# A fused group-norm, sign convolution and involution kernel: lane swaps in place of statistics matmuls, a second sum bank, whole copies on ScalarE, and patch loads put in another order

## What is computed

```python
x = x + conv3x3(sign(gn(x)), sign(weight)) * scale      # gn: mean and variance over each pair of channels
r   = relu(bn(w_r @ gn(x) + b_r))                       # 64 channels to 16
ker = w_s @ r + b_s                                     # 16 channels to 49 taps x 16 groups, for every pixel
for ki in range(7):
    for kj in range(7):                                 # the "involution": a 7x7 kernel of its own at every pixel
        out = out + pad(gn(x))[:, ki:ki+56, kj:kj+56] * ker[ki*7+kj]     # one kernel for the 4 channels of a group
x = x + out
```

## Time and profile before

| | us |
|---|---|
| median of 3 runs | 2095.22 (2088.94 to 2097.33) |
| profiled execution, its own time | 2100.36 |
| its span, first to last instruction | 2097.7 |
| PE busy | 1703.9 (81%) |
| DVE busy | 1350.2 (64%) |
| ACT busy | 1056.1 (50%) |
| POOL busy | 1025.0 (49%) |
| granted TensorE clock, mean | 0.914 |

### The profile page before, as it was taken

One profiled execution on the slowest core, in us unless ns is written; L12 is line 12 of the kernel. 1 busy time (PEld: TensorE's weight loads), 2 busy tenths in 40 slices (PEclk: granted clock), 3 DMA queues, 4 the chain that ended last, 5 costly groups with the idle time before them and its releaser, 6 DMA issues.

```text
span 2097.7 us, 39368 instructions
## 1 busy us (share of the span) xinstructions
PE 1703.9 (81%) x15168; PEld 752.8 (36%) x15168; DVE 1350.2 (64%) x1652; ACT 1056.1 (50%) x758; POOL 1025.0 (49%) x905
## 2 busy tenths in 40 slices
PE   3487887888788788887878888788887878878775
PEld 2243333433333333333333333333333433333332
DVE  5376665757667575776657667576766757667574
ACT  2354555544555445555545555445555545554453
POOL 2145455444545444555454545445555454544573
PEclk8798999999989899999989999899998999989997
DMA  4679789797898978899797997978799798997894
GB/s 102 171 184 225 202 229 227 183 232 198 223 210 206 230 192 222 199 236 238 185 234 185 236 225 200 227 195 229 194 233 230 190 228 198 235 225 185 211 259 110
DMA packets 224283, 436.47 MB, mean 208 GB/s; under 512 B 89214, under 2 KB 136751, under 8 KB 219951
## 3 DMA queue, kind: packets, MB, share of 16 engines
q1 hardware_dynamic: 148832, 382.57, 73.7%
q10 hardware_dynamic: 75264, 51.39, 9.8%
HBM read 336.06 MB, written 84.93 MB: 201 GB/s over the span
## 4 chain that ended last, share of the span: by engine, by line
issue 38%; POOL 37%; PE 9%; SPq 7%; DMA 3%; DVE 2%; ACT 2%; POOLq 0%; ACTq 0%; DVEq 0%
POOL folded L369 37%; SPq L307 5%; PE ybank L564 3%; PE ybank L583 2%; DMA patches<-parts_dram 2%; PE obank L594 1%; DVE prod L820 1%; SPq L289 1%; DMA relu<-blocks 1%; PE ybank L554 1%; PE ybank L525 1%; PE obank L601 1%; PE ybank L615 1%; ACT blocks L458 0%; ACT blocks L416 0%
## 5 line engine op out<-in xcount | busy, mean ns | idle before, releaser
L369 POOL TENSOR_TENSOR folded<-prod 128x448 f32<-128x448 f32 x896 | 1013.3, 1144 | 1051.0 <-DVE prod L820 1040.6
L820 DVE TENSOR_TENSOR prod<-ybank,relu 128x896 f32<-128x896 f32 x896 | 956.8, 1086 | 314.2 <-PE ybank L583 240.2
L583 PE MATMUL ybank<-patches,wspan 128*64 128x448 f16 x7168 | 845.5, 374 | 157.2 <-DVE prod L820 128.5
L436 ACT ACTIVATE patches<-patches 64x1792 f16<-64x1792 f16 x448 | 740.9, 1698 | 450.0 <-DMA patches<-parts_dram 228.5
L583 PEld LDWEIGHTS ybank<-patches,wspan 128*64 128x64 f16 x7168 | 370.5, 114 | 657.7 <-DVE prod L820 256.8
L594 PE MATMUL obank<-patches,wbias 128*32 128x448 f16 x3584 | 223.4, 399 | 80.1 <-ACT osb L424 80.1
L601 PE MATMUL obank<-folded,esum 128*32 128x448 f32 x1792 | 225.7, 577 | 1.5 <-POOL folded L369 1.5
L525 PE MATMUL ybank<-sgn,convw 128*128 128x448 bf16 x1008 | 207.3, 359 | 12.7 <-ACT sgn L389 7.6
L594 PEld LDWEIGHTS obank<-patches,wbias 128*32 128x32 f16 x3584 | 93.3, 105 | 199.0 <-ACT osb L424 95.7
L832 DVE TENSOR_TENSOR xs<-ybank,xs 128x1024 f32<-128x1024 f32 (+1 forms) x64 | 61.9, 967 | 142.1 <-PE ybank L615 142.1
L615 PE MATMUL ybank<-back,blocks 128*128 128x128 f32 (+1 forms) x448 | 70.5, 310 | 101.1 <-ACT blocks L458 101.1
(11 more groups left out here) (92 smaller groups left out, 447.3 us busy)
## 6 DMA issues: line engine op xcount, KB each, us to landing
patches<-parts_dram SPq DMA_DIRECT2D x1232, 224.0 KB, 6.4
parts_dram<-parts SPq DMA_DIRECT2D x128, 256.0 KB, 3.4
xs<-x_dram SPq DMA_DIRECT2D x128, 196.0 KB, 4.7
sums_dram<-osb ACTq DMA_DIRECT2D x112, 224.0 KB, 5.7
rows<-sums_dram ACTq DMA_DIRECT2D x112, 224.0 KB, 5.0
out_dram<-xs SPq DMA_DIRECT2D x128, 196.0 KB, 3.7
relu<-blocks SPq DMA_DIRECT2D x256, 49.0 KB
patches<-gb_dram SPq DMA_DIRECT2D x1, 784.0 KB
```

The source lines that it names most:

```text
L369: pool.tensor_tensor(folded[:, u % 8, :], prod[:, u % 2, 0, :], prod[:, u % 2, 1, :], ALU.add).then_inc(fold_done, 1)
L436: act.activation(X2[0:COPIED_ROWS, e % 2, at], X1[0:COPIED_ROWS, e % 3, at], ACT.Copy).then_inc(copied, 1)
L583: mm = pe.matmul(bank("unit", p, n)[64 * t:64 * t + 64, h, 0:N], wspan[0:STACK_ROWS[stack], stack, g, h, :], of_group(e, stack, g), start= ...
L820: dve.tensor_tensor(prod[:, u % 2].rearrange("m h (n c) -> m h n c", c=GC), bank("unit", p, n)[:, :, 0:N].rearrange("m h (n c) -> m h n c" ...
```

## The change

Five things change together.

1. **Lane swaps.** The `stat` matmuls, `gmat`, its load and `mbank` go. DVE gets the other channel of a pair by `stream_shuffle` (partition i reads i ^ 1), and works out mean and variance alone (`negative_mean`, `variance`). The steps move: sign from unit 7 to 5, mean from 5 to 4, variance from 21 to 18 (with the part that was at 19), the root on ACT from 23 to 18, `affine` from 22 to 20, `normalize` from 23 to 21.
2. **Two sum banks.** Strips use `obank` 0 and 1 in turn; `bias(e)` waits for `o_read` of strip e-2.
3. **Full copies.** `copy_high` copies all 128 rows of X1 to X2, at units 0 to 3 of the strip before instead of 0, 1, 4, 5. Five planes of X2 are what was copied; `second_stack` loads 2 planes over copied rows, so it waits for the copies (`copied`). The clearing of X2 at the start goes. A strip takes 10 planes.
4. **Loads.** The first plane of X1 is loaded by two DMAs of eight rows, ahead of and behind the seven others. `first_stack(e+2)` is issued ahead of `second_stack(e+1)`, at the start of the kernel `spread(0)` ahead of `second_stack(0)`.
5. **Outputs.** The `outputs` of strips 0 to 3 move from units 46 and 49 to 50 and 53 (from strip 5 to strip 6), their `arrange` from 43 to 46.

```diff
-PLANES = (((0, 0, 0, 4), (0, 4, 64, 4), (0, 1, 1, 4), (1, 0, 65, 4),
-           (0, 2, 2, 4), (1, 1, 66, 4), (0, 3, 3, 4), (1, 2, 67, 4)),
-          tuple((0, a, a, 4) for a in range(4)) + ((0, 4, 64, 4), (1, 3, 65, 4), (1, 4, 66, 4)))
-COPIED_ROWS, COPIED_PLANES = 64, 4
+PLANES = (((0, 0, 0, 4), (0, 3, 64, 4), (0, 1, 1, 4), (0, 4, 65, 4),
+           (0, 2, 2, 4), (1, 1, 66, 4), (1, 0, 3, 4), (1, 2, 67, 4)),
+          ((0, 0, 0, 4), (0, 3, 64, 4), (0, 1, 1, 4), (0, 4, 65, 4),
+           (0, 2, 2, 4), (1, 4, 66, 4), (1, 3, 3, 4)))
+COPIED_PLANES = 5
...
-OUT0_AT = {46: 0, 49: 1}
-ARRANGE1_AT, ARRANGE0_AT = 13, 43
+OUT0_AT = {50: 0, 53: 1}
+ARRANGE1_AT, ARRANGE0_AT = 13, 46
...
-COPY_AT = {0: 0, 1: 1, 4: 2, 5: 3}
+COPY_AT = {0: 0, 1: 1, 2: 2, 3: 3}
...
             def first_stack(e):
...
-                for l, a, row, step in PLANES[0]:
+                def half(r):
+                    l, a, row, step = PLANES[0][0]
+                    sp.dma_start(X1[row + step * r:row + step * r + 7 * step + 1:step, e % 3, :],
+                                 plane(e, l, a, r, 8)).then_inc(first_in[e % 3], 16)
+                half(0)
+                for l, a, row, step in PLANES[0][1:]:
                     sp.dma_start(X1[row:row + 15 * step + 1:step, e % 3, :],
                                  plane(e, l, a)).then_inc(first_in[e % 3], 16)
+                half(8)
             def second_stack(e):
+                sp.wait_ge(copied, JX * (e + 1))
                 if e >= 2:
-                    sp.wait_ge(y_ready, GP * (e - 1))
                     sp.wait_ge(second_in[e % 2], SECONDLOAD * (e // 2))
...
             first_stack(0)
+            spread(0)
             second_stack(0)
-            spread(0)
             first_stack(1)
             for p in range(pairs):
                 for s in range(E):
                     e = E * p + s
+                    if e + 2 < EALL:
+                        first_stack(e + 2)
                     if e + 1 < EALL:
                         second_stack(e + 1)
-                    if e + 2 < EALL:
-                        first_stack(e + 2)
...
-                act.activation(X2[0:COPIED_ROWS, e % 2, at], X1[0:COPIED_ROWS, e % 3, at],
-                               ACT.Copy).then_inc(copied, 1)
+                act.activation(X2[:, e % 2, at], X1[:, e % 3, at], ACT.Copy).then_inc(copied, 1)
...
             def bias(e, stack):
-                if stack == 0 and e > 0:
-                    pe.wait_ge(o_read, e)
+                if stack == 0 and e >= 2:
+                    pe.wait_ge(o_read, e - 1)
...
             def negative_mean(p):
-                dve.wait_ge(stat_ready, 3 * p + 1)
-                dve.tensor_scalar(col(S_NMEAN), Mbank[:, 0:1], -1.0 / HW, None, ALU.mult).then_inc(stat_read, 1)
...
+                link(dve.stream_shuffle(other[:, 0:1], col(S_SUM), OTHER))
+                link(dve.tensor_tensor(both[:, 0:1], col(S_SUM), other[:, 0:1], ALU.add))
+                dve.tensor_scalar(col(S_NMEAN), both[:, 0:1], -0.5 / HW, None, ALU.mult).then_inc(nmean_ready, 1)
```

More of the change, by code:

```diff
@@ L19 @@
 HALVES, OH = 2, 8
+OTHER = [i ^ 1 for i in range(32)]
 K, PAD = 7, 3
@@ L51 @@
 C_ID, C_SEL = 0, 128
-C_G = C_SEL + POS * 384
-C_E = C_G + 128
+C_E = C_SEL + POS * 384
 C_R = C_E + 48
@@ L150, in build @@
         Ybank = [ctx.enter_context(nc.psum_tensor(f"ybank{i}", [128, 2, 512], F32)) for i in range(3)]
-        Obank = ctx.enter_context(nc.psum_tensor("obank", [128, 512], F32))
-        Mbank = ctx.enter_context(nc.psum_tensor("mbank", [128, 512], F32))
+        Obank = [ctx.enter_context(nc.psum_tensor(f"obank{i}", [128, 512], F32)) for i in range(2)]
         D = nc.dram_tensor("parts_dram", (2, 2, 128, PART), F16, kind="Internal").ap()
@@ L244, in build @@
         (S_SUM, S_NMEAN, S_GM, S_D, S_T, S_VE, S_SD, S_Y, S_U, S_RS, S_NB) = range(11)
+        other, both = sm[:, 30:32], sm[:, 32:34]
         def cols(i, n):
@@ L273, in parts_out, with plane @@
                                  Ev[:, l, k % 2]).then_inc(d_written[k], 16)
-            def plane(e, l, a):
+            def plane(e, l, a, r=0, many=16):
                 p = e // E
                 first = ((p % 2) * 2 + l) * 128 * PART + 4 * JX * (e % E) * PART
-                return bass.AP(tensor=D.tensor, offset=first + (a % 2) * (CY // 2) * 128 + (a // 2) * 128,
-                               ap=[[PART, 16], [4 * PART, JX], [1, JY * 128]])
+                return bass.AP(tensor=D.tensor, offset=first + (a % 2) * (CY // 2) * 128 + (a // 2) * 128 + r * PART,
+                               ap=[[PART, many], [4 * PART, JX], [1, JY * 128]])
             def first_stack(e):
@@ L423, in gather @@
                     act.wait_ge(sums_written, 16 * e)
-                act.activation(osb[:], Obank[:, 0:N], ACT.Copy, scale=alpha[:]).then_inc(o_read, 1)
+                act.activation(osb[:], Obank[e % 2][:, 0:N], ACT.Copy, scale=alpha[:]).then_inc(o_read, 1)
                 act.wait_ge(o_read, e + 1)
@@ L486, in _ @@
                         rows(e - 1)
-                    if more and n == STAT0_AT:
+                    if more and n == SIGN_AT:
                         sign(p + 1)
-                    if more and n == STAT2_AT:
+                    if more and n == ROOT_AT:
                         root(p + 1)
+                    if more and n == NORMAL_AT:
                         normalize(p + 1)
@@ L505, in turn @@
                     pe.wait_ge(*read_by(*TURNS[i - 3]))
-            def stat(p, n):
-                if n == 0:
-                    pe.wait_ge(sum_ready, p + 1)
-                    rhs = col(S_SUM)
-                else:
-                    pe.wait_ge(stats_ready, 2 * p + n)
-                    rhs = mv[:, 0:1] if n == 1 else col(S_T)
-                if 3 * p + n > 0:
-                    pe.wait_ge(stat_read, 3 * p + n)
-                pe.matmul(Mbank[:, 0:1], gmat[:], rhs, start=True, stop=True).then_inc(stat_ready, 1)
             def conv(p, k):
@@ L541, in select_bias @@
                     sel, n = t_sel16[:, pos], 32 * pos
-                    pe.matmul(Obank[:, n:n + 16], sel[:, 0, :], t_b16[:, 0, :], start=True, stop=True)
-                    pe.matmul(Obank[:, n + 16:n + 32], sel[:, 1, :], t_b16[:, 0, :], start=True, stop=False)
-                    mm = pe.matmul(Obank[:, n + 16:n + 32], sel[:, 2, :], t_b16[:, 1, :], start=False, stop=True)
+                    pe.matmul(Obank[0][:, n:n + 16], sel[:, 0, :], t_b16[:, 0, :], start=True, stop=True)
+                    pe.matmul(Obank[0][:, n + 16:n + 32], sel[:, 1, :], t_b16[:, 0, :], start=True, stop=False)
+                    mm = pe.matmul(Obank[0][:, n + 16:n + 32], sel[:, 2, :], t_b16[:, 1, :], start=False, stop=True)
                 mm.then_inc(bsel_ready, 1)
@@ L569, in of_group @@
                 at = (X1[:, e % 3, :], X2[:, e % 2, :])[stack]
-                return at[0:STACK_ROWS[stack]].rearrange("k (j g n) -> k g j n", g=GROUPS, n=8)[:, g]
+                return at.rearrange("k (j g n) -> k g j n", g=GROUPS, n=8)[:, g]
             def taps(p, n):
@@ L593, in bias @@
                         g = 4 * t + i
-                        pe.matmul(Obank[32 * t:32 * t + 32, 0:N], wbias[0:STACK_ROWS[stack], stack, g, :],
+                        pe.matmul(Obank[e % 2][32 * t:32 * t + 32, 0:N], wbias[:, stack, g, :],
                                   of_group(e, stack, g), start=(stack == 0 and i == 0), stop=False)
@@ L648, in _ @@
                         sums(e, 0)
-                    if more and n == STAT0_AT:
-                        stat(p + 1, 0)
                     if more and n in CONV_AT:
@@ L654, in _ @@
                         outputs(p - 1, 2 + OUT1_AT[n])
-                    if more and n == STAT1_AT:
-                        stat(p + 1, 1)
-                    if more and n == STAT2_AT:
-                        stat(p + 1, 2)
                     if more and n in T_AT:
```

62 lines of the change are left out of this document (20 added, 42 removed).

## The result

| | median us | runs from, to | to the kernel before, 95% interval |
|---|---|---|---|
| before, same chip | 2092.84 | 2088.94 to 2097.33 | 1 |
| the change | 2147.2 | 2145.11 to 2152.07 | 1.0262 (1.0232 to 1.0292) |

The change is 2.6% slower; 2152 us was forecast. First the page, its head and the loads, and then the groups of the copies (L442) and the bias (L589) with the idle time ahead of them.

The account below looks back on a forecast made before the run. Loads near the DMA engines' limit, and their order, were taken to bound it: 129.4 against 126.1 us a pair, +49 us for 15 pairs, +5 end, +3 start, giving 2157, less 5.1: 2152 us; range 2065 to 2190.

Parts of the forecast that it names:

- S2 to S4: From start of a pair's strip 2 to strip 4: 35.0 us, set by loads behind the stores; 1.1 us less than before.
- S4 to S6: From strip 4's start to strip 6's: 44.5 us, 4.7 us more, as strip 6's loads come behind spread and nine DMAs.
- S6 to S0: From strip 6's start to the next pair's strip 0: 14.3 us, 1.3 less, with two loads issued after the fourth copy.
- S0 to S1: From strip 0's start to strip 1's: 13.6 us against 12.3, as two DMAs land behind the copies and first stack.
- S1 to S2: From strip 1's start to strip 2's: 22.0 us, bounded by PE's own work, 0.3 us less for the statistics matmul.
- The order of the loads: Behind the spread, strip 6's two loads follow nine others, last issued 37.7 us after strip 4 starts; +4.7 us a pair.
- The shorter strip 2 is thus eaten by strip 3: Lane swaps shorten strip 2 to near 16.5 us, but loads behind the stores hold strip 4's start to 1.1 us sooner.
- The step on the banks: Two sum banks remove 80.1 us of wait, 5 us a pair, mostly in strips 5, 6 and 0, ahead of the next landing.
- The waits: PE's first taps wait 100 to 250 us for patches; its waits for blocks and sum bank nearly go; SP waits for copies.
- The halves: First plane's two eight-row DMAs cost 0.99 us each on half the engines; at 0.5 us each, 45 us less: 2107.
- Start and end: Strips 0 and 1 at the kernel's start cost +3 us; the last pair's six strips, without preparation, +5 us.
- The clock term: Waits at starts of strips 4, 5 and 6 lower PE's clock; strip 4 losing 1.5 us adds 22 us, giving 2175.

Follow-up runs that it names:

- experiments 7 and 8: 7: the change without its full copies and loads, 2017.33 us, ratio 0.9602; 8: the same with first stack issued ahead of second stack, 2166.43 us, ratio 1.0338.
- experiment 6: Lane swaps and two sum banks alone: the change without full copies, its loads and order, outputs as before; 2025.0 us, ratio 0.9643.
- experiment 5: The kernel before with only the outputs of strips 0 to 3 moved to units 50 and 53, their arrange to 46; 2092.01 us, ratio 0.9966.
- experiment 4: The change with the outputs back at units 46 and 49 and their arrange at 43; 2153.24 us, ratio 1.0245.
- experiment 3: The change with each of the first plane's two DMAs carrying all 16 rows and half the columns; 2134.66 us, ratio 1.0176.

## Why the prediction was right, point by point

The table sets the terms against the means over 14 pairs.

| stretch | forecast | measured | before |
|---|---|---|---|
| S2 to S4 | 35.0 | 33.7 | 35.8 |
| S4 to S6 | 44.5 | 45.8 | 39.8 |
| S6 to S0 | 14.3 | 15.4 | 15.6 |
| S0 to S1 | 13.6 | 12.5 | 12.5 |
| S1 to S2 | 22.0 | 21.8 | 22.7 |
| pair | 129.4 | 129.2 | 126.4 |

**The order of the loads** is the cause, and shown: alone it costs 1.0338/0.9602 = 7.7% (experiments 7 and 8), and S4 to S6 goes from 39.3 to 48.0 us by it (means). The mechanism came as forecast, the terms a little short: in the mean the last issue ends 38.3 us after S4, not 37.7, and S6 is 7.5 us behind it, not 6.8 to 7.2. One load is missing from the sum of this stretch: ACT's `rows` reads 224 KB of sums back here (L454 at 1099.07), in each of the 14 pairs 3.6 to 3.7 us after the first issue. At 231 GB/s it is 1.0 us of the DMA engines by estimate; the forecast counts such sums from S2 to S4 only. Both ways of the copies and the order are measured, all with lane swaps, banks and outputs as in the change:

| | old order | new order |
|---|---|---|
| copies of 64 rows, 8 + 3 planes | 0.9602 | 1.0338 |
| full copies (halves in both) | 1.1695 | 1.0262 |

Together the copies and loads cost 1.0262/0.9602 = 6.9%. In the new order the full copies (with the halves) give 0.7% back; in the old they cost 22%. They need the new order, and it costs more than they give.

**"The shorter strip 2 is thus eaten by strip 3"** is the weakest step. Strip 2 didn't get shorter: 18.4 us against 18.3 before, where "near 16.5" was forecast from one long strip of 19.6. What the lane swaps give stands in strip 3, which PE no longer spends waiting for late products. Strip 3 loses 2.2 us in the change (17.5 to 15.3), and without the new order 5.2 (experiment 6). The lane swaps and the banks are worth 3.6% where the loads allow it; the prediction priced them under the new order only. The step on the banks, that their wait "stands ahead of the next strip's start, which the landing of the next strip's patches now sets", holds for the change only. How the 3.6% divide between swaps and banks wasn't tried. The strips say that most stands in strip 3, where DVE's wait was; S6 to S0, where PE waited for the sum bank, gives 1.6 us, and S4 to S6 takes 2.1 more (experiment 6).

**The waits** moved to the place that was forecast, but the first taps' wait for patches is 346.7 us when both rows are counted, above the range of 100 to 250. That the outputs' wait was no loss of its own is shown from both sides: moving them gives 0.3% before (experiment 5), 0.4% with the old loads (0.9602 against 0.9643), and nothing in the change (experiment 4).

**The halves.** The price of 0.99 us each isn't borne out. The Trainium skill's rule ("DMA: Bandwidth & Descriptors", section "Why a DMA increments its semaphore by 16 and not by 1") puts each eight-row DMA on the eight lowest-numbered of the 16 engines; an even spread was to be 45 us less. The halves by columns are 0.8% less, some 18 us; the whole plane is not less at all. So neither price is borne out by the times. The traces' packets speak for fewer engines, though not for which: of the first 32 patch packets (3584 bytes each) behind a spread, at most 9 to 11 are under way at once in the change, and at most 14 to 18 in experiment 3, whose two DMAs have 16 rows each (14 pairs of both). What eight rows cost in time stays open.

**Full copies** cost nothing on ACT: 1696 ns in the earlier trace rows and 1696 ns now. **S6 to S0 and S0 to S1** erred by 1.1 us each to opposite sides, and so did S2 to S4 and S4 to S6, by 1.3. The errors cancel, and that the pair's sum came out at 129.2 for 129.4 is luck. **Start and end:** the second pair starts 4.2 us later (+3 was forecast), and the last pair's six strips take 4.5 us more (+5). The clock term, +22 us if strip 4 lost 1.5 us, didn't come. Strip 4 did lose 0.9 us (20.2 against 19.3), at a granted clock of 0.96 against 1.00, and 0.7 us of wait for patches at its end is in that. But the spread's issue ends no later for it: 30.9 us after S4, and 31.1 before (means).

## What to carry to other kernels

A wait that a trace shows large may only cover another one: look for what would be waited for at the same place if it went, here the loads, and price that. In one DMA queue, what is needed next goes first. Behind a prefetch for later it waits for the issue and the transfer of all of it. And an edit (here the full copies) that makes the urgent load wait for other work pushes it behind the prefetch. Price such edits apart: two of the five here gained 3.6%, another two lost 6.9%, and the sum hid both.

## What the runs showed of the hardware

A shuffle of one or two columns on DVE takes 0.15 us, but the small instruction behind it 1.06. The groups by line and shape of the change:

```profile
L769 DVE TENSOR_TENSOR small<-mv,small 128x2 f32<-128x2 f32 x16 | 16.9, 1056 | 0.6
...
L768 DVE STREAM_SHUFFLE small<-mv 128x2 f32<-128x2 f32 x16 | 2.4, 152 | 0.0
```

Others as small take 0.16 us. The cause wasn't tried; the kernel before has a small product of 1.06 us as well (the first of `inv_root`, L680), with no shuffle anywhere, so the shuffle needn't be it. The spread's small DMAs of 16 rows, SBUF to SBUF, take their issuer 0.72 to 0.77 us each, on SP or on ACT, against 0.63 us for a plane of 224 KB. The Trainium skill ("Trainium Kernel Development and Optimization", section "Key Constraints") says that issuing from several engines only saves the sequencer's issue time; here that saving was bought with 11.5 us in which ACT did nothing else, and 82 us were lost.
